# Causal attention inside a four-layer hybrid kernel: query preparation and normalising on GpSimd, and the mask of the maxima added by VectorE

## The chip, the cores and the metric

The kernel runs on one core of a Trainium2 chip. The metric is the device time of one execution in microseconds, lower is better. The core's engines are named as in the profile: PE (TensorE, matrix products), DVE (VectorE), ACT (ScalarE), POOL (GpSimd) and SP (SyncE, which here only issues transfers). They run their own instruction streams and meet at semaphores.

## The reference

Four layers follow each other, each `x = x + layer(layernorm(x))` on `x` of 4 x 1024 tokens of 128: a fast-weight attention, a mixture of experts, a causal attention, and the mixture of experts again. The change lies in the third. There `x` is seen as 2 batches of 256 in the layer's own text, but the shapes come from the argument, so it runs on 4 batches of 1024 tokens, with 16 heads of 8:

```python
def proj(W, b):
    y = jnp.einsum('bth,oh->bto', x, W) + b
    return y.reshape(B, T, nh, hs).transpose(0, 2, 1, 3)
Q, K, V = proj(Wq, bq), proj(Wk, bk), proj(Wv, bv)
Q = _apply_rope(Q, cos, sin)     # cos*even - sin*odd, the odd places zero
K = _apply_rope(K, cos, sin)
scores = jnp.einsum('bhqd,bhkd->bhqk', Q, K) * (1.0 / jnp.sqrt(hs))
scores = jnp.where(causal, scores, -10000000000.0)
att = jax.nn.softmax(scores, axis=-1)
y = jnp.einsum('bhqk,bhkd->bhqd', att, V)
return jnp.einsum('bth,oh->bto', y, Wo) + bo
```

## The kernel before, in words

`causal_attention_stage` is one block of five engine programs. A batch's 16 heads are four quads (`QUADS`, `QUAD`). Because the odd places after the rotation are zero, a head's rotated query and key have four numbers each (`ROT`). `rotate` multiplies the even half by the cosines and the odd half by the sines, `split` subtracts and writes the result as three bf16 parts; three `split`s give parts whose products add up to fp32 accuracy. ScalarE stacks the parts into rows (`stack_queries`, `stack_keys`), PE transposes the rows of a quad, and SP's transfers place the keys of each head (`place_keys`).

**Two passes over the scores.** The softmax needs the maximum of each query. So for each quad the scores are computed twice. First with the queries on the partitions: `max_step` makes a product of up to 512 keys in one of two PSUM buffers (`ps1`), and VectorE reduces it to one maximum (`maxima`, L1829, semaphores `s1_done` and `max_done`). A block of 128 queries j and a chunk c of 512 keys is a step; 12 steps (`MAX_STEPS`) of four heads make a quad, and in 8 of the 12 the last 128 columns lie on the diagonal: there a second product of the identity with a mask of -1e30 adds the causal mask (L1722). GpSimd splits the negated maxima in three bf16 parts too (`stack_maxima`) and they ride in the queries' rows, so that the second product gives score minus maximum. That one has the keys on the partitions (`exp_step`, two heads at a time in `ps2`, masked by a product as well, L1734); ScalarE takes the exponential, and `value_step` multiplies by the values in fp32.

**The slots.** A slot is one quad's 12 exponential steps. The maxima run ahead: step n of a slot also does maximum step n + 4 (`LEAD`) of the next quad, or, from n = 8 on, n - 8 of the one after. Within a step PE's order is: maximum product of head 0, exponential products of the first pair, head 1, second pair, head 2, then what stands under (n, "mid"), the value products of step n - 1, head 3, then what stands under (n, "end"). VectorE's order is the four reductions with the same places between. A maximum product waits until the buffer's last maximum but one is reduced (`max_done`), so each engine can be two maxima ahead of the other at most.

**The tables.** `COMMON`, `PREP`, `VALUES` and `OUTPUT` name what is done at the places: transposes of keys ("k") and queries ("q1", "q2"), of the output ("o0", "o1"), of the normalised input ("x0", "x1"), projections ("qk0" to "qk3", "v0", "v1"). All share one spare bank (`psm`) through `misc_full` and `misc_free`: who fills it waits until the last content was copied out, by ScalarE for k, q1, q2 and x, by VectorE for the rest.

**Preparing the next batch** is done in the slot of quad 1 (`prep`), in a loop over three batches; batch 0 is prepared before the first slot. VectorE takes the statistics of the layer norm at n = 1, GpSimd makes 1/sqrt(var + eps) (`rsqrt`), VectorE normalises at n = 3 (`normalize`, L1853: eight operations of 128 x 128), PE needs the result (`xn_done`) at "x0". After "qk3" VectorE rotates q (n = 10) and splits it in three pieces, at n = 11 and at n = 0 and 1 of the next slot, while GpSimd rotates and splits k. ScalarE waits for `q_split` at n = 2 and for `k_split` at n = 3 of quad 2's slot.

## Time and profile before

| | us |
|---|---|
| median of 3 runs | 1774.78 |
| lowest, highest run | 1768.44, 1775.36 |
| the profiled execution | 1769.27 |
| its span, first to last instruction | 1767.2 |
| attention stage in it, about | 787 to 1500 |

Times within a profile are microseconds from the span's start. A row of a timeline gives start, length, engine, line and operation, what it writes and reads, how many instructions were merged in it, and in brackets how long the engine had been idle before it and what released it. The length of merged instructions runs from the start of the first to the end of the last, and consecutive instructions of an engine overlap at their ends. Over the whole span PE is busy 69%, DVE 58%, ACT 36% and POOL 29%; these are averages over four layers with different limits, so the attention stage has to be read by itself.

### The profile page before, as it was taken

Reading aid. Unit: us, or ns where it says so; the run is one execution under the profiler, and the core shown is the slowest. Engines: PE = TensorE matmul, PEld = TensorE weight load, DVE = VectorE, ACT = ScalarE, POOL = GpSimd, SP = SyncE. Lnnn points to the kernel's source line nnn. Section 1 sums busy time; section 2 is a strip of 40 time slices with the busy share of each in tenths; the row PEclk is TensorE's granted clock in tenths of the full one; section 3 lists DMA queues with packets and bytes.
Section 4 is the critical chain, followed back from the end, with each engine's and each line's share of the span. In section 5 each row is a group of like instructions: output and inputs, shape, how many; then the busy total and the mean of one; then the engine's idle time right before and its main releaser. Section 6 shows DMA issues by size and latency. Waiting matters only on the chain. (4 is left out here: it accounts for less than half of the span.)

```text
span 1767.2 us, 26688 instructions
## 1 busy us (share of the span) xinstructions
PE 1212.8 (69%) x9140; PEld 801.2 (45%) x9214; DVE 1021.9 (58%) x2340; ACT 629.5 (36%) x989; POOL 510.0 (29%) x571
## 2 busy tenths in 40 slices
PE   4625977959635059704888998899889997412991
PEld 2413856839524059702343443344434443311991
DVE  5855555655426136446777776777777770630662
ACT  4632221222111023201265664665566665001330
POOL 2434013040026747712003000300120000374772
PEclk9666988969755579955699998999999998555995
DMA  1439611020120133160000010001000100213325
GB/s 45 155 145 390 266 37 59 0 95 0 36 63 28 53 106 99 52 185 6 7 19 7 10 46 8 7 7 43 8 7 8 31 7 13 62 53 90 98 68 162
DMA packets 109057, 114.06 MB, mean 65 GB/s; under 512 B 8720, under 2 KB 90512, under 8 KB 108048
## 3 DMA queue, kind: packets, MB, share of 16 engines
q1 hardware_dynamic: 96608, 91.98, 16.5%
q0 software_dynamic: 9216, 19.02, 3.2%
q10 hardware_dynamic: 3120, 1.57, 0.3%
q8 instruction: 68, 1.11, 0.3%
q14 instruction: 45, 0.37, 0.1%
HBM read 49.34 MB, written 59.02 MB: 61 GB/s over the span
## 5 line engine op out<-in xcount | busy, mean ns | idle before, releaser
L1829 DVE TENSOR_REDUCE att_mx<-att_ps 128x1 f32<-128x512 f32 (+3 forms) x768 | 405.2, 555 | 146.9 <-PE att_ps L1722 111.3
L1603 ACT ACTIVATE att_prob<-att_ps 128x1024 f32<-128x1024 f32 (+3 forms) x384 | 300.3, 812 | 228.9 <-PE att_ps L1734 176.7
L1719 PE MATMUL att_ps<-att_kT,att_q1T 128*128 128x512 bf16 (+3 forms) x709 | 235.1, 344 | 50.5 <-DVE att_mx L1829 34.2
L1731 PE MATMUL att_ps<-att_q2T,att_kT 128*128 128x512 bf16 (+3 forms) x753 | 201.1, 331 | 3.2 <-ACT att_prob L1603 1.2
L1719 PEld LDWEIGHTS att_ps<-att_kT,att_q1T 128*128 128x128 bf16 x768 | 74.2, 98 | 259.1 <-DVE att_mx L1829 211.7
L978 POOL DMA_INDIRECT sides<-moe_ys,moe_back_i x160 | 153.2, 958 | 87.6 <-issue 47.3
L1745 PE MATMUL att_pso<-att_prob,att_v 128*32 128x512 f32 (+3 forms) x1536 | 163.9, 499 | 1.6
L972 POOL DMA_INDIRECT slots<-moe_rows,moe_place_i x128 | 123.2, 963 | 59.4 <-issue 38.4
L1499 POOL CAST att_qm_rows<-att_nm 128x32 bf16<-128x32 f32 x48 | 15.6, 324 | 395.8 <-DVE att_nm L1838 391.6
L1722 PE MATMUL att_ps<-att_mask,att_identb 128*128 128x128 bf16 x512 | 115.8, 228 | 2.3 <-DVE att_mx L1829 1.5
L1071 PE MATMUL moe_ps_t<-moe_ident,moe_xs 128*128 128x128 f32 x160 | 27.0, 290 | 115.2 <-DMA moe_xs<-slots 115.2
L1734 PE MATMUL att_ps<-att_mask,att_identb 128*128 128x128 bf16 x512 | 102.4, 221 | 1.4 <-ACT att_prob L1603 0.8
L1018 ACT ACTIVATE moe_gated<-moe_ps_g 128x512 f32<-128x512 f32 (+1 forms) x96 | 50.6, 527 | 131.0 <-PE moe_ps_u L1086 131.0
L1265 DVE TENSOR_TENSOR moe_hid<-moe_gated,moe_ps_u 128x512 f32<-128x512 f32 (+1 forms) x96 | 57.4, 598 | 64.0 <-ACT moe_gated L1018 62.4
L1731 PEld LDWEIGHTS att_ps<-att_q2T,att_kT 128*128 128x128 bf16 x768 | 72.3, 99 | 47.7 <-ACT att_prob L1603 13.2
L1096 PE MATMUL moe_ps_y<-expert_wd,moe_hid 128*128 128x128 f32 x640 | 78.8, 275 | 0.0
L1096 PEld LDWEIGHTS moe_ps_y<-expert_wd,moe_hid 128*128 128x128 f32 x640 | 77.5, 191 | 2.7
L1071 PEld LDWEIGHTS moe_ps_t<-moe_ident,moe_xs 128*128 128x128 f32 x160 | 20.6, 151 | 115.8 <-issue 115.5
L1009 ACT ACTIVATE moe_xT_hi<-moe_ps_t 128x512 fp32r<-128x512 f32 (+1 forms) x48 | 25.1, 522 | 127.3 <-PE moe_ps_t L1071 127.3
L461 POOL TENSOR_TENSOR fw_wn<-fw_ssq,fw_half 128x20 f32<-128x20 f32 x3 | 10.6, 3532 | 202.1 <-DVE fw_ssq L668 202.1
L1230 DVE SCALAR_TENSOR_TENSOR moe_empty<-moe_xs,moe_spare_token 128x5 f32<-128x5 f32 x32 | 5.4, 176 | 109.7 <-DMA moe_xs<-slots 109.7
L696 DVE TENSOR_TENSOR fw_A<-fw_banks,fw_block_ones 128x512 f32<-128x512 f32 x45 | 31.1, 692 | 62.9 <-PE fw_banks L630 62.9
(283 smaller groups left out, 2439.5 us busy)
## 6 DMA issues: line engine op xcount, KB each, us to landing
slots<-fw_zeros SPq DMA_DIRECT2D x2, 5200.0 KB, 30.1
moe_xs<-slots SPq DMA_DIRECT2D x16, 650.0 KB, 4.9
sides<-fw_zeros SPq DMA_DIRECT2D x2, 4096.0 KB, 35.3
moe_side<-sides SPq DMA_DIRECT2D x16, 512.0 KB, 6.2
tok<-prep_tok SPq DMA_DIRECT2D x4, 1536.0 KB, 5.4
turned<-prep_tT SPq DMA_DIRECT2D x4, 1536.0 KB, 8.7
fw_tok<-tok SPq DMA_DIRECT2D x4, 1536.0 KB, 10.4
fw_Tkv<-turned SPq DMA_DIRECT2D x4, 1024.0 KB, 6.7
```

Source lines behind the costliest of these rows:

```text
L972: pool.indirect_dma_start(slots, bass.IndirectOffsetOnAxis(ap=place_i[b][:, j, k:k + 1], axis=0), source, None).then_inc(slots_written, 16)
L978: pool.indirect_dma_start(sides, bass.IndirectOffsetOnAxis(ap=back_i[e % 2][:, j:j + 1], axis=0), ys[n % 4][:, j - first], None).then_inc( ...
L1018: nc.scalar.activation(gated[k][:, 0:size], ps_g[k][:, 0:size], ACT.Silu).then_inc(silu_done, 1)
L1096: last = nc.tensor.matmul(ps_y[n % 2][:, j], hid[n % 2][k][:, j * P:(j + 1) * P], wd[:, e, k], start=(k == 0), stop=(k == 1))
L1265: nc.vector.tensor_tensor(hid[n % 2][k][:, 0:size], gated[k][:, 0:size], ps_u[k][:, 0:size], ALU.mult).then_inc(hid_done, 1)
L1603: nc.scalar.activation(prob[(2 * n + pair) % 4][:, :, 0:size], ps2[pair][:, :, 0:size], ACT.Exp, scale=SCORE_SCALE).then_inc(exp_done, 1)
L1719: last = nc.tensor.matmul(out[:, 0:size], q1T[t % 2][:, j * P:(j + 1) * P], kT[t][h][:, 512 * c:512 * c + size], start=True, stop=not diag ...
L1722: last = nc.tensor.matmul(out[:, size - P:size], identb[:], mask[:, 0], start=False, stop=True)
L1731: last = nc.tensor.matmul(ps2[pair][:, h, 0:size], kT[t][2 * pair + h][:, i * P:(i + 1) * P], q2T[t % 2][:, first:first + size], start=Tru ...
L1734: last = nc.tensor.matmul(ps2[pair][:, h, 0:P], identb[:], mask[:, 1], start=False, stop=True)
L1745: last = nc.tensor.matmul(pso[32 * h:32 * h + 32, first:512], v1[:, i * HEADS + QUAD * t + h, :], prob[(2 * n + h // 2) % 4][:, h % 2, 0:5 ...
L1829: nc.vector.reduce_max(mx[:, c, j, h:h + 1], ps1[(n * QUAD + h) % 2][:, 0:size], AX.X).then_inc(max_done, 1)
```

## The change

Four things are done at once.

1. `rsqrt` on GpSimd goes on to normalise, eight `tensor_scalar`s into `xn`, and gives `xn_done` itself. `rstd_done` and VectorE's `normalize` go, for batch 0 too.
2. In the loop GpSimd rotates and splits q, then k, where it did k alone. VectorE's pieces for q go. For batch 0 the work stays divided as before.
3. Statistics are taken at n = 0, and "x0" to "qk3" move one step forward in `PREP`.
4. Maxima on the diagonal: the mask product goes from PE. VectorE uses `tensor_tensor_reduce`, which adds a row block `mask_end` (384 zeros, then the mask's 128 columns) to the scores, writes the sums back to PSUM and keeps their maximum. `mask_end` is filled once at the start. In the built program this is two instructions, the second of which reads the maximum out. Before each maximum, on the diagonal or not, the wait is an instruction of its own (`wait`), which also counts up a semaphore.

```diff
-        PREP = {(4, "mid"): "x0", (5, "mid"): "x1", (7, "mid"): "qk0", (8, "mid"): "qk1", (9, "mid"): "qk2", (10, "mid"): "qk3"}
+        PREP = {(3, "mid"): "x0", (4, "mid"): "x1", (6, "mid"): "qk0", (7, "mid"): "qk1", (8, "mid"): "qk2", (9, "mid"): "qk3"}
...
-                nc.gpsimd.tensor_tensor(rstd[:], vareps[:], negh[:], ALU.pow).then_inc(rstd_done, 1)
+                nc.gpsimd.tensor_tensor(rstd[:], vareps[:], negh[:], ALU.pow)
+                pool.drain()
+                for j in range(TILES):
+                    last = nc.gpsimd.tensor_scalar(xn[:, j], xb[:, j], mv[:, j, 0:1], rstd[:, j:j + 1], ALU.subtract, ALU.mult)
+                last.then_inc(xn_done, 1)
...
-                    rotate(nc.gpsimd, 1)
-                    for n in range(3):
-                        last = split(nc.gpsimd, 1, n)
-                    last.then_inc(k_split, 1)
+                    for k, done in ((0, q_split), (1, k_split)):
+                        rotate(nc.gpsimd, k)
+                        for n in range(3):
+                            last = split(nc.gpsimd, k, n)
+                        last.then_inc(done, 1)
...
-                    last = nc.tensor.matmul(out[:, 0:size], q1T[t % 2][:, j * P:(j + 1) * P], kT[t][h][:, 512 * c:512 * c + size],
-                                            start=True, stop=not diagonal)
-                    if diagonal:
-                        last = nc.tensor.matmul(out[:, size - P:size], identb[:], mask[:, 0], start=False, stop=True)
-                    last.then_inc(s1_done, 1)
+                    nc.tensor.matmul(out[:, 0:size], q1T[t % 2][:, j * P:(j + 1) * P], kT[t][h][:, 512 * c:512 * c + size],
+                                     start=True, stop=True).then_inc(s1_done, 1)
...
-                    dve.wait_ge(s1_done, G * (STEPS * QUAD) + (n * QUAD + h + 1))
-                    nc.vector.reduce_max(mx[:, c, j, h:h + 1], ps1[(n * QUAD + h) % 2][:, 0:size], AX.X).then_inc(max_done, 1)
+                    wait(dve, s1_done, G * (STEPS * QUAD) + (n * QUAD + h + 1))
+                    scores, largest = ps1[(n * QUAD + h) % 2][:, 0:size], mx[:, c, j, h:h + 1]
+                    if P * (j + 1) == 512 * c + size:
+                        nc.vector.tensor_tensor_reduce(scores, scores, mask_end[:, 512 - size:512], 1.0, MASKED, ALU.add, ALU.max, largest).then_inc(max_done, 1)
+                    else:
+                        nc.vector.reduce_max(largest, scores, AX.X).then_inc(max_done, 1)
...
-                    if S.prep and n == 1:
+                    if S.prep and n == 0:
                         statistics(S.b + 1)
-                    if S.prep and n == 3:
-                        normalize(S.b + 1)
-                    if S.prep and n == 10:
-                        dve.drain()
-                        rotate(nc.vector, 0)
-                    if S.prep and n == 11:
-                        split(nc.vector, 0, 0)
-                    if S.t == 2 and S.more2 and n < 2:
-                        last = split(nc.vector, 0, n + 1)
-                        if n == 1:
-                            last.then_inc(q_split, 1)
...
+            nc.vector.memset(mask_end[:, 0:512 - P], 0.0)
+            nc.vector.tensor_copy(mask_end[:, 512 - P:512], mask_f[:, 0])
```

GpSimd in the loop's prepared slot, from the last cast of the maxima on: before, k alone (`att_turned`, `att_parts` are written once for k).

```order
L1505 ISA
L1415 REGISTER_ALU
L1464 TENSOR_TENSOR att_turned<-att_qkv,att_cs 128x512 x2
L1470 TENSOR_TENSOR att_turned<-att_turned 128x512
L1472 CAST att_parts<-att_turned 128x128x4
L1470 TENSOR_TENSOR att_turned<-att_turned,att_parts 128x512
L1472 CAST att_parts<-att_turned 128x128x4
L1470 TENSOR_TENSOR att_turned<-att_turned,att_parts 128x512
L1472 CAST att_parts<-att_turned 128x128x4
L1415 ISA
L1509 TENSOR_TENSOR att_res<-att_res,att_bo 128x1024
```

After the change the same place begins with q's five kinds of rows, and k's follow.

```order
L1473 CAST att_parts<-att_turned 128x128x4
L1471 TENSOR_TENSOR att_turned<-att_turned,att_parts 128x512
L1473 CAST att_parts<-att_turned 128x128x4
L1465 TENSOR_TENSOR att_turned<-att_qkv,att_cs 128x512 x2
L1471 TENSOR_TENSOR att_turned<-att_turned 128x512
L1473 CAST att_parts<-att_turned 128x128x4
L1471 TENSOR_TENSOR att_turned<-att_turned,att_parts 128x512
L1473 CAST att_parts<-att_turned 128x128x4
```

These are the end of q's rows and the beginning of k's: k's first multiplication stands behind all of q's, and the addition to `att_res` behind both.

PE in the same slot, from the transposes of the keys to the first projection. Before, the queries' transposes lie between the keys' transposes and qk0 (L1707), and a mask product (`att_mask,att_identb`) follows each maximum of a diagonal step. The piece shown begins at the queries' transposes; qk0 comes one more maximum later.

```order
L1667 MATMUL att_psm<-att_identb,att_q_rows 128x128 x8
L1718 REGISTER_ALU
L1719 MATMUL att_ps<-att_kT,att_q1T 128x512
L1722 MATMUL att_ps<-att_mask,att_identb 128x128
L1729 REGISTER_ALU
L1731 MATMUL att_ps<-att_q2T,att_kT 128x512 x2
L1718 REGISTER_ALU
L1719 MATMUL att_ps<-att_kT,att_q1T 128x512
L1722 MATMUL att_ps<-att_mask,att_identb 128x128
```

After:

```order
L1673 MATMUL att_psm<-att_identb,att_k_rows 128x128 x8
L1723 REGISTER_ALU
L1724 MATMUL att_ps<-att_kT,att_q1T 128x512
L1731 REGISTER_ALU
L1733 MATMUL att_ps<-att_q2T,att_kT 128x512 x2
L1723 REGISTER_ALU
L1724 MATMUL att_ps<-att_kT,att_q1T 128x512
L1731 REGISTER_ALU
L1733 MATMUL att_ps<-att_q2T,att_kT 128x512 x2
L1723 REGISTER_ALU
L1724 MATMUL att_ps<-att_kT,att_q1T 128x512
L1702 REGISTER_ALU
L1713 MATMUL att_psm<-att_wqkv,att_xT 128x256 x2
```

qk0 (now L1713) stands three maxima behind the keys' transposes, in the same bank; before, it stood three maxima behind the queries' transposes. The products with `att_mask` are gone from the maxima.

VectorE at the start of that slot. Before, the statistics stand behind the second step's maxima:

```order
L1828 REGISTER_ALU
L1829 TENSOR_REDUCE att_mx<-att_ps 128x1
L1842 ISA
L1844 BN_STATS att_stats<-att_xb 128x6 x8
L1847 BN_AGGR att_mv<-att_stats 128x2 x8
L1828 REGISTER_ALU
L1829 TENSOR_REDUCE att_mx<-att_ps 128x1
```

After, they stand behind the first step's, and the diagonal maxima that follow are pairs, an add-maximum (`att_ps,att_mx<-att_ps,att_mask_end`) and a read-out (`att_mx`):

```order
L1835 TENSOR_REDUCE att_mx<-att_ps 128x1
L1848 ISA
L1850 BN_STATS att_stats<-att_xb 128x6 x8
L1853 BN_AGGR att_mv<-att_stats 128x2 x8
L1416 REGISTER_ALU
L1833 ISA att_ps,att_mx<-att_ps,att_mask_end 128x128
L1833 ISA att_mx 128x1
L1416 REGISTER_ALU
L1833 ISA att_ps,att_mx<-att_ps,att_mask_end 128x128
L1833 ISA att_mx 128x1
```

The reduction before was one instruction with its wait inside; the waits, which this listing doesn't show, are now instructions between the rows.

## Rows read from the trace of the kernel before

**Rows 1.** Page, part 2: busy tenths of 40 slices of 44.2 us

```profile
PEclk9666988969755579955699998999999998555995
```

**Rows 2.** DVE by form: line, form, xcount | busy us, mean ns | idle

```profile
L1829 DVE TENSOR_REDUCE att_mx<-att_ps 128x1 f32<-128x512 f32 x384 | 253.2, 688 | 52.1 <-PE att_ps L1719 24.8 <-PE att_ps L1722 23.1
...
L1829 DVE TENSOR_REDUCE att_mx<-att_ps 128x1 f32<-128x256 f32 x128 | 53.0, 422 | 27.2 <-PE att_ps L1722 23.2
...
L696 DVE TENSOR_TENSOR fw_A<-fw_banks,fw_block_ones 128x512 f32<-128x512 f32 x45 | 31.1, 692 | 62.9 <-PE fw_banks L630 62.9
L701 DVE SCALAR_TENSOR_TENSOR fw_T<-fw_A,fw_eyes 128x512 f32<-128x512 f32 x45 | 30.8, 685 | 1.4
```

**Rows 3.** Timeline of PE in a plain step of 256 columns

```profile
1189.08 0.27 PE L1719 MATMUL att_ps<-att_kT,att_q1T 128*128 128x256 bf16 x1
1189.19 0.22 PE L1722 MATMUL att_ps<-att_mask,att_identb 128*128 128x128 bf16 x1
...
1190.94 0.28 PE L1719 MATMUL att_ps<-att_kT,att_q1T 128*128 128x256 bf16 x1
...
1191.80 0.34 PE L1719 MATMUL att_ps<-att_kT,att_q1T 128*128 128x384 bf16 x1
```

**Rows 4.** Timeline of DVE: maxima, aggregations, and a small operation

```profile
1079.86 0.64 DVE L1847 BATCH_NORM_AGGREGATE att_mv<-att_stats 128x2 f32<-128x6 f32 x8
...
1122.65 2.53 DVE L1829 TENSOR_REDUCE att_mx<-att_ps 128x1 f32<-128x512 f32 x4
...
1186.18 0.17 DVE L1833 TENSOR_TENSOR att_mx<-att_mx 128x16 f32<-128x16 f32 x1
1186.43 0.18 DVE L1838 TENSOR_SCALAR att_nm<-att_mx 128x32 f32<-128x32 f32 x1
...
1191.32 2.02 DVE L1829 TENSOR_REDUCE att_mx<-att_ps 128x1 f32<-128x256 f32 x4 [0.84 <-PE att_ps L1722]
```

**Rows 5.** Timeline of PE: its long waits for DVE in preparing slots

```profile
955.43 0.39 PE L1719 MATMUL att_ps<-att_kT,att_q1T 128*128 128x512 bf16 x1 [1.46 <-DVE att_mx L1829]
...
1088.42 0.60 PE L1701 MATMUL att_psm<-att_ident,att_xn 128*128 128x128 f32 x4 [2.06 <-DVE att_mx L1829]
...
1118.82 0.39 PE L1719 MATMUL att_ps<-att_kT,att_q1T 128*128 128x512 bf16 x1 [2.09 <-DVE att_mx L1829]
...
1128.21 0.23 PE L1719 MATMUL att_ps<-att_kT,att_q1T 128*128 128x128 bf16 x1 [2.25 <-DVE att_mx L1829]
```

**Rows 6.** Timeline of DVE: the preparing work of batch 1

```profile
1085.40 2.14 DVE L1853 TENSOR_SCALAR att_xn<-att_xb,att_mv,att_rstd 128x128 f32<-128x128 f32 x8
...
1110.58 0.69 DVE L1870 TENSOR_TENSOR att_qkv<-att_psm,att_bias 128x512 f32<-128x512 f32 x1 [0.49 <-PE att_psm L1707]
...
1125.28 2.18 DVE L1470 TENSOR_TENSOR att_turned<-att_turned,att_parts 128x512 f32<-128x512 f32 x1
```

**Rows 7.** Timeline of POOL: rstd, k's rotation and split, a cast

```profile
1081.09 1.67 POOL L1486 TENSOR_TENSOR att_rstd<-att_vareps,att_negh 128x8 f32<-128x8 f32 x1 [0.15 <-issue]
...
1115.10 2.52 POOL L1464 TENSOR_TENSOR att_turned<-att_qkv,att_cs 128x512 f32<-128x512 f32 x2 [8.02 <-DVE att_qkv L1870]
...
1123.99 0.61 POOL L1472 CAST att_parts<-att_turned 128x512 bf16<-128x512 f32 x1
...
1186.78 0.32 POOL L1499 CAST att_qm_rows<-att_nm 128x32 bf16<-128x32 f32 x1 [28.04 <-DVE att_nm L1838]
```

**Rows 8.** Stretch: us, PE, PEld, DVE, ACT, POOL busy (x), PEclk, DMA share, GB/s

```profile
1080.00:1120.00 40.00, 32.99 (x249) 16.21 (x254) 29.33 (x67) 18.33 (x25) 8.82 (x12) 0.96 0.03 8
```

**Rows 9.** POOL by form, as rows 2

```profile
L1472 POOL CAST att_parts<-att_turned 128x512 bf16<-128x512 f32 x12 | 8.4, 703 | 1.6
...
L1484 POOL TENSOR_SCALAR att_vareps<-att_mv 128x8 f32<-128x8 f32 x4 | 1.0, 242 | 60.3 <-DVE att_mv L1847 60.3
```

**Rows 10.** Timeline of ACT: the first stacking of k

```profile
1135.71 1.47 ACT L1587 ACTIVATE att_k_rows<-att_parts 128x1536 bf16<-128x1536 bf16 x1
```

**Rows 11.** Waits of PE, 1080 to 1150: total us, times, longest

```profile
PE att_psm L1707 <- ACT att_q1T L1558: 1.1, 1, 1.1
```

More of the change, by code:

```diff
@@ L1301, in causal_attention_stage @@
         mask = sb("mask", [P, 2, P], BF16)
+        mask_end = sb("mask_end", [P, 512])
         cs = sb("cs", [P, TILES, 2, ROT])
@@ L1342, in causal_attention_stage @@
         x_loaded, res_loaded, res_biased, x_stored = sem("x_loaded"), sem("res_loaded"), sem("res_biased"), sem("x_stored")
-        stats_done, rstd_done, xn_done, q_split, k_split = sem("stats_done"), sem("rstd_done"), sem("xn_done"), sem("q_split"), sem("k_split")
+        stats_done, xn_done, q_split, k_split = sem("stats_done"), sem("xn_done"), sem("q_split"), sem("k_split")
         q_stacked, k_stacked, q_copied, k_placed, v_placed = sem("q_stacked"), sem("k_stacked"), sem("q_copied"), sem("k_placed"), sem("v_placed")
@@ L1716, in max_step @@
                     out = ps1[(n * QUAD + h) % 2]
-                    diagonal = P * (j + 1) == 512 * c + size
                     pe.wait_ge(max_done, u + 1)
-                    last = nc.tensor.matmul(out[:, 0:size], q1T[t % 2][:, j * P:(j + 1) * P], kT[t][h][:, 512 * c:512 * c + size],
-                                            start=True, stop=not diagonal)
-                    if diagonal:
-                        last = nc.tensor.matmul(out[:, size - P:size], identb[:], mask[:, 0], start=False, stop=True)
-                    last.then_inc(s1_done, 1)
+                    nc.tensor.matmul(out[:, 0:size], q1T[t % 2][:, j * P:(j + 1) * P], kT[t][h][:, 512 * c:512 * c + size],
+                                     start=True, stop=True).then_inc(s1_done, 1)
             def exp_step(G, t, n, pair):
@@ L1848, in statistics @@
                 last.then_inc(stats_done, 1)
-            def normalize(batch):
-                dve.wait_ge(rstd_done, batch + 1)
-                for j in range(TILES):
-                    last = nc.vector.tensor_scalar(xn[:, j], xb[:, j], mv[:, j, 0:1], rstd[:, j:j + 1], ALU.subtract, ALU.mult)
-                last.then_inc(xn_done, 1)
             def consume(use, count, t, batch):
@@ L1918, in _ @@
             nc.vector.memset(k_rows[:], 0.0)
-            normalize(0)
             for zeros in [q_rows] + qm_rows:
```

## The prediction

> **What bounds the kernel now.** First the page's strip of the granted clock [rows 1]: the attention stage lies in slices 19 to 33, about 820 to 1460 us, and there the clock is 9 tenths or more in nearly all slices (2.4 GHz). Outside the stage the change touches nothing. A stretch of it shows PE busy 33 of 40 us and DVE 29 [rows 8]; matmul ends are modelled, so that doesn't settle who waits. Next comes a timeline of one plain step [rows 3, 4].
>
> A step on PE is: max product 0, exp pair 0, max 1, exp pair 1, max 2, value products, max 3. Max 1 of the next step writes the PSUM buffer of this step's max 3, so it waits for DVE's reduction of that. In the step of 256 columns, max 1 starts at 1189.08, max 3 at 1190.94, DVE's reduction at 1191.32, and the next max 1 at 1191.80. The reduction takes 0.42 [rows 2], so it ends at 1191.74 and PE moves 0.06 later. The loop of 2.72 us is 1.86 of PE work, 0.38 from max 3 to DVE, 0.42 of DVE and 0.06 back. PE idles only about 0.15 of it: the stage is bound by a loop through both engines, with PE alone a short way behind. DVE alone is further behind: four reductions of 512 in a row take 2.53 [rows 4], so they start (2.53 - 0.69) / 3 = 0.61 apart, 2.45 for a widest step.
>
> Then the slots that prepare the next batch. There PE stops for DVE: 2.06 us for xn, 2.09 and 2.25 behind q's rotation and split, and 1.46 for the same in batch 0 [rows 5]. DVE's own rows name the work [rows 6]: 2.14 us of normalising, and one subtraction that took 2.18.
>
> **The change, part by part.** The sum is made against the profiled execution, 1769.3 us (span 1767.2). The runs' median, 1774.8, is 5.5 above it and the fastest run 0.8 below; I forecast on the profile's scale.
>
> *Normalising leaves DVE (3 loop batches).* PE's wait of 2.06 goes if GpSimd has xn in time. Before, GpSimd had rstd at 1082.76 [rows 7]. The statistics that it waits for, of 1079.86 [rows 4], now come a step (3 us) earlier: rstd at 1079.8. The eight tensor_scalars on GpSimd aren't in the trace. The nearest rows are 242 ns for 8 elements and 703 ns for a cast of 512 [rows 9]: by elements 0.35 each, 2.8 in all, at most 5.6. So xn is there at 1082.6, and PE wants x0 a step earlier than before, 1086.36 - 3.0 = 1083.4. No wait; with 5.6 a wait of 2.0, as before. Taken: -2.06 x 3 = -6.2, range -6.2 to 0. At the stage's start nothing hides it, and 2.8 stands for 2.14: +0.7 (up to +3.5).
>
> *q's rotation and split leave DVE.* PE's stops of 2.09 and 2.25 fall away, and a third: batch 0 shows 1.46, while batch 1 instead ran that stretch at 1.2 GHz, which took as much. 5.80 x 3 = -17.4. Batch 1 also fell to 1.2 GHz after its wait for xn; its 40 us window has a mean of 0.96 of full clock [rows 8], which is 3.2 us at half speed and costs 1.6: -1.6 once.
>
> *GpSimd does q, then k.* For k it took from 1115.10 to 1124.60, 9.5 us [rows 7]; its start waits for the last qk projection, which is now read a step earlier, when qk2 was (1110.58 + 0.69 [rows 6]). So q is done near 1120.9 and k near 1130.4, with a margin since DVE no longer runs beside it. ScalarE took k at 1135.71 [rows 10]; less the stops that go (5.8) it wants it at 1129.9. q has over 3 us in hand, k is late by 0.5: +1.5 for three batches, range 0 to +6. Behind that wait on ScalarE stand the exponentials, and PE and DVE behind those. add_output_bias and the next queries' copy, queued behind k on GpSimd, aren't needed before.
>
> *The projections move a step earlier.* qk0 now follows k's transposes in the one spare PSUM bank, not q1's. PE waited 1.1 us for ScalarE to copy q1 out before qk0 [rows 11]. Now it does so twice, after k and after q1: +1.2 x 3 = +3.6 (0 to +3.9).
>
> *PE loses 512 mask products.* Each holds PE 0.06 (1189.19 to the next product, 0.05 by its 128 columns) [rows 3]. The loop holds three of them (max 1, 2 and 3): -0.16 a step.
>
> *DVE's maximum becomes a wait, an add-maximum and a read-out.* The add-maximum reads PSUM and SBUF; an addition or product of that form takes 692 ns for 512, the reduction 688 [rows 2], so the main instruction is even. The read-out of one element isn't in the trace. From below: eight aggregations take 0.64 with 0.152 each, so 0.07 apart [rows 4]. From above: the small operation at 1186.43 starts 0.25 after its predecessor's start at 1186.18, behind a drain. I take 0.07, because nothing drains between; it comes before max_done, so it is in the loop. The wait is now an instruction of its own for every maximum: from 0 to 0.17 (GpSimd, which waits in this way, starts its cast at 1186.78, 0.17 after nm's end at 1186.61 [rows 4, 7]). I take 0.02, since it only shows when DVE is early.
>
> There are 192 steps of four maxima, 128 on the diagonal; 16 (12 diagonal) are in the prologue, where I count 0. In the rest: 116 x (-0.16 + 0.07) = -10.4, the waits 176 x 0.02 = +3.5. Where the widest maxima meet the shortest exponentials, the same loop with that step's widths comes to 2.65 (an estimate, a column at 1/2.4 ns), while DVE alone needs 4 x 0.70 = 2.8: +0.15 in each of 14 slots, +2. Together -5; break-even at 0.16 for read-out and wait.
>
> Sum: 1769.3 - 6.2 + 0.7 - 17.4 - 1.6 + 1.5 + 3.6 - 5 = 1744.9.
>
> Two-source vector operations on fp32 run at one element a cycle here, with one source in PSUM (692 ns) and with both in SBUF (685) [rows 2]. Neither keeps an accumulator. The Trainium skill, Vector Engine (DVE) Microarchitecture Reference, section Points that are easy to get wrong, says that scalar-tensor-tensor with two non-bf16 SBUF sources runs at half throughput, as no port is left for accumulator read-back. No row here shows that form, and the new one has only one source in SBUF; by the rule as it is written the sum stands, by its reason the second rival would come.
>
> **The rivals.**
> *Read-out and wait at their upper bounds.* 0.25 + 0.17 against 0.16 saved: +0.26 x 116 = +30, and the 60 other steps at +0.17 = +10: 1769.3 - 19.4 (all but the masks) + 40 = **1790**. With the wait at 0.05 the kernel is slower than before from a read-out of 0.26 on ((0.26 + 0.05 - 0.16) x 116 + 0.05 x 60 = 20). For it: two rows of that size. Against: both have a drain or another engine in them.
> *The add-maximum at half rate.* Then 512 elements cost 0.53 more, 384 0.40, 256 0.27. DVE alone would bind: 4 x 1.23 = 4.9 a step against loops of 3.1 and 2.7 for the two widest, 3.9 against 3.0 and 2.7, 2.8 against 2.2 and 2.6 (estimates, as above): with the narrow ones +7 a slot, in 176 / 12 = 14.7 slots, +103: 1769.3 - 19.4 + 103 = **1853**. Against: the 692 and 685 ns. The reason of the skill's rule just named would give this time.
> *GpSimd is late.* xn at its upper price (PE waits 2.0) and k 1 us later, three times: +9: **1754**. This is the new wait in the place of the one removed. For it: both margins are under 1 us.
> *PE alone binds the diagonal steps*, and all four masks count: 116 x -0.21 = -24, and no more than that from DVE: 1769.3 - 19.4 - 24 = **1726**. For it: PE idles only 0.15 in the step shown; against: the loop still has the 0.07.
>
> **How the numbers follow.** Forecast 0.52, upper bounds 0.16, half rate 0.06, GpSimd late 0.14, PE alone 0.12. Predicted 1745 us. Half rate and the top of the first rival are left out of the range: 1727 to 1775. Half a per cent (9 us, about what a measurement of this kernel can tell) from the median 1774.8: below 1766 lie forecast, GpSimd late and PE alone, 0.78, less 0.02 for the unforeseen, 0.76; of the first rival's 0.16 half is within, so same 0.10; slower 0.14.
>
> **What would show it.** Right: no PE wait over 1.5 us for DVE in preparing slots, two waits of about 1.2 before projections; add-maxima of about 690 ns at 512, followed by rows that start 0.6 after them and end by 0.76; plain slots 0.4 us shorter. Wrong: add-maxima near 1.2 us; plain slots longer than before; PE waiting for xn, or ScalarE for k; a granted clock under 1.0 in plain slots, since PE has less to do.

## The result: 0.4% slower, and the profile after

The changed kernel takes 1777.75 us in the median against 1771.54 for the kernel before on the same chip (15 runs each). The ratio is 1.0037, with a 95% interval of 1.0026 to 1.0047. Its profiled execution took 1778.23 us with a span of 1776.3, 9 more than the 1769.27 and 1767.2 of before. Forecast was 1745, with a range that ended at 1775: wrong in sign and outside the range.

The clock strip of after's page stands at 9 tenths or more in slices 20 to 33, where [rows 1] has two slices of 8. Falls of a few microseconds don't show in slices of 44 us:

```profile
PEclk8666988969755579855699999999999999555996
```

VectorE's maxima in after, by form over the whole span (columns as in [rows 2]):

```profile
L1835 DVE TENSOR_REDUCE att_mx<-att_ps 128x1 f32<-128x512 f32 x256 | 172.8, 690 | 39.8 <-PE att_ps L1724 32.7 <-remote 2.2 <-issue 1.8
L1833 DVE CUSTOM_DVE_ANT_0 att_ps<-att_ps,att_mask_end 128x512 f32<-128x512 f32 x128 | 87.9, 704 | 13.1 <-PE att_ps L1724 10.1
L1833 DVE DVE_READ_ACCUMULATOR2_ANT att_mx<- 128x1 f32 x512 | 72.4, 141 | 0.1
```

The add-maximum of 512 columns takes 704 ns, not the 1.2 us of the half-rate rival. Two in a row in the timeline of DVE, in a plain slot of after:

```profile
1189.13 0.70 DVE L1833 CUSTOM_DVE_ANT_0 att_ps<-att_ps,att_mask_end 128x512 f32<-128x512 f32 x1
1189.75 0.14 DVE L1833 DVE_READ_ACCUMULATOR2_ANT att_mx<- 128x1 f32 x1
1189.78 0.70 DVE L1833 CUSTOM_DVE_ANT_0 att_ps<-att_ps,att_mask_end 128x512 f32<-128x512 f32 x1
1190.40 0.14 DVE L1833 DVE_READ_ACCUMULATOR2_ANT att_mx<- 128x1 f32 x1
1190.53 0.70 DVE L1833 CUSTOM_DVE_ANT_0 att_ps<-att_ps,att_mask_end 128x512 f32<-128x512 f32 x1
```

The read-out starts 0.62 after the main instruction and ends 0.76 after it, as forecast (0.6 and 0.76). So neither the half rate nor a dear read-out came, yet plain slots became longer. The negated maxima are taken once a slot. Their rows give, for each kernel, first and last start (columns: line, engine, operation, count: shortest, median, longest ns, first and last start in us). In this order they are before, after, and six of the kernels below: waits, mask, no_product, q_norm, q_only, early.

```profile
L1838 DVE TENSOR_SCALAR att_nm<-att_mx x16: 181/181/182, 861.4 to 1457.0; 128x32 f32<-128x32 f32 x16
L1844 DVE TENSOR_SCALAR att_nm<-att_mx x16: 181/181/182, 869.1 to 1467.2; 128x32 f32<-128x32 f32 x16
L1838 DVE TENSOR_SCALAR att_nm<-att_mx x16: 181/181/182, 863.5 to 1478.6; 128x32 f32<-128x32 f32 x16
L1839 DVE TENSOR_SCALAR att_nm<-att_mx x16: 181/181/182, 868.0 to 1480.5; 128x32 f32<-128x32 f32 x16
L1834 DVE TENSOR_SCALAR att_nm<-att_mx x16: 181/181/183, 859.0 to 1450.0; 128x32 f32<-128x32 f32 x16
L1843 DVE TENSOR_SCALAR att_nm<-att_mx x16: 181/181/183, 864.6 to 1451.1; 128x32 f32<-128x32 f32 x16
L1839 DVE TENSOR_SCALAR att_nm<-att_mx x16: 181/181/182, 860.0 to 1447.8; 128x32 f32<-128x32 f32 x16
L1839 DVE TENSOR_SCALAR att_nm<-att_mx x16: 181/181/182, 862.4 to 1432.3; 128x32 f32<-128x32 f32 x16
```

The sixteen starts cut the stage into fifteen intervals. Eight are plain (no preparing, clock at 1.00 in all kernels) and tell the price of the masks. The seven kernels whose plain slots have the same code (before, q_norm, q_only, start_dve, table_back, early and spread) lie between 293.3 and 295.0 there, so a price can be read to about 0.2 a slot. Three pairs hold the preparing of a batch. "First maximum" and "first negated" are counted from the stage's first statistics. q_only2 is a second run of the kernel q_only.

| us | first maximum | first negated | first to last | eight plain intervals | the three preparing pairs |
|---|---|---|---|---|---|
| before | 45.7 | 76.5 | 595.7 | 293.4 | 86.0, 93.0, 89.1 |
| after | 50.0 | 82.4 | 598.1 | 300.5 | 83.0, 89.2, 88.4 |
| waits | 45.8 | 78.9 | 615.1 | 303.7 | 88.2, 93.0, 92.8 |
| waits2 | 45.9 | 81.5 | 631.8 | 312.3 | 91.4, 95.2, 94.6 |
| mask | 45.7 | 79.3 | 612.5 | 300.8 | 88.0, 93.3, 93.4 |
| no_product | 45.6 | 74.8 | 591.0 | 285.8 | 85.8, 92.3, 92.7 |
| after_nd | 50.0 | 82.4 | 592.5 | 296.6 | 82.8, 88.8, 87.4 |
| q_norm | 50.0 | 80.8 | 586.5 | 293.3 | 82.0, 88.6, 86.7 |
| q_only | 45.7 | 76.5 | 587.8 | 294.9 | 84.4, 86.1, 88.2 |
| q_only2 | 45.7 | 77.0 | 589.1 | 295.0 | 84.4, 87.8, 86.0 |
| start_dve | 45.7 | 75.2 | 591.2 | 294.8 | 82.0, 90.5, 88.7 |
| table_back | 45.7 | 76.5 | 591.5 | 295.0 | 83.2, 88.8, 88.6 |
| early | 45.8 | 76.5 | 569.8 | 294.8 | 77.7, 81.2, 80.3 |
| spread | 45.7 | 75.2 | 574.0 | 294.3 | 78.8, 83.2, 82.4 |

In after, then: +4.3 before the first maximum, +1.7 more to the first negated one, +7.1 in eight plain intervals (0.89 each), +2.8 in the first interval, where full clock is granted from 885 on instead of 871, and -7.5 in the three pairs with the masks' share in them, where without it -20 was forecast. The first interval also differs by 1.6 between the two profiles of the one kernel q_only, so its +2.8 is no firm price. The profiled execution also reached the stage 1.8 later than before's, and was 1.2 quicker behind the last negated maxima, both in code that is the same. Together that is the 9 us of the span.

PE's long waits in the preparing slot of batch 1, from the timeline of PE in after (they answer to [rows 5]):

```profile
1087.63 0.23 PE L1724 MATMUL att_ps<-att_kT,att_q1T 128*128 128x128 bf16 x1 [1.83 <-DVE att_mx L1833]
1096.13 0.54 PE L1707 MATMUL att_psm<-att_ident,att_xn 128*128 128x128 f32 x3 [2.44 <-POOL att_xn L1490]
1108.02 0.70 PE L1713 MATMUL att_psm<-att_wqkv,att_xT 128*128 128x256 f32 x2 [1.17 <-ACT att_kT_all L1571]
1113.59 0.48 PE L1713 MATMUL att_psm<-att_wqkv,att_xT 128*128 128x256 f32 x1 [1.06 <-ACT att_q1T L1564]
1155.25 0.23 PE L1724 MATMUL att_ps<-att_kT,att_q1T 128*128 128x128 bf16 x1 [0.84 <-DMA att_kT<-att_kT_all]
```

The stops of 2.09 and 2.25 behind q's work are gone. The two waits of about 1.2 before projections are there. But PE still waits for xn, now for GpSimd: 2.44 here, and 1.00 in each of the other two batches. The first row is the stop behind the statistics. It was 1.69 in before too, once a batch, and the prediction's list of stops lacks it.

### The profile page after: what moved, and what is told of

It is laid out like the page before. It is cut to its first block and busy times, and to the rows that moved or that the text cites. A ratio compares the mean times of both kernels' runs of the same rounds, so it can differ in the third digit from the quotient of the medians.

```text
span 1776.3 us, 26950 instructions
## 1 busy us (share of the span) xinstructions
PE 1202.1 (68%) x8635; PEld 778.6 (44%) x8702; DVE 1027.1 (58%) x2798; ACT 631.0 (36%) x989; POOL 554.9 (31%) x627
## 5 line engine op out<-in xcount | busy, mean ns | idle before, releaser
L1833 DVE CUSTOM_DVE_ANT_0 att_ps<-att_ps,att_mask_end 128x384 f32<-128x384 f32 (+3 forms) x512 | 250.8, 501 | 105.9 <-PE att_ps L1724 94.6
L1835 DVE TENSOR_REDUCE att_mx<-att_ps 128x1 f32<-128x512 f32 x256 | 172.8, 690 | 39.8 <-PE att_ps L1724 32.7
L1736 PE MATMUL att_ps<-att_mask,att_identb 128*128 128x128 bf16 x512 | 102.2, 221 | 1.1 <-ACT att_prob L1609 0.8
L1733 PEld LDWEIGHTS att_ps<-att_q2T,att_kT 128*128 128x128 bf16 x768 | 74.4, 98 | 40.1 <-ACT att_prob L1609 13.2
L1096 PE MATMUL moe_ps_y<-expert_wd,moe_hid 128*128 128x128 f32 x640 | 78.8, 275 | 0.0
L1833 DVE DVE_READ_ACCUMULATOR2_ANT att_mx<- 128x1 f32 x512 | 72.4, 141 | 0.1
```

The costliest lines, as they stand in the source:

```text
L1096: last = nc.tensor.matmul(ps_y[n % 2][:, j], hid[n % 2][k][:, j * P:(j + 1) * P], wd[:, e, k], start=(k == 0), stop=(k == 1))
L1733: last = nc.tensor.matmul(ps2[pair][:, h, 0:size], kT[t][2 * pair + h][:, i * P:(i + 1) * P], q2T[t % 2][:, first:first + size], start=Tru ...
L1736: last = nc.tensor.matmul(ps2[pair][:, h, 0:P], identb[:], mask[:, 1], start=False, stop=True)
L1833: nc.vector.tensor_tensor_reduce(scores, scores, mask_end[:, 512 - size:512], 1.0, MASKED, ALU.add, ALU.max, largest).then_inc(max_done, 1)
L1835: nc.vector.reduce_max(largest, scores, AX.X).then_inc(max_done, 1)
```

## Experiments on the masks and the waits

Ratios are to the kernel before on the same chip, with their 95% intervals. The chip of after_nd, waits2, start_dve and table_back ran the kernel before in 1847.8 us instead of 1771, so those four are compared by ratio, or by the intervals of the stage. The kernel before has no profile from that chip.

**mask**: the kernel before with item 4 alone. 

> The kernel before with the mask part of the change alone: mask products off PE, add-maximum and read-out on VectorE, a wait of its own before each maximum. Theory (read-out and wait outweigh the products saved): in the trace of after the plain slots are 0.8 us longer than before and the prologue up to the first negated maxima 1.7 longer, so 14.7 x 0.8 + 1.7 = +13 against the kernel before. Rival (my prediction's term): -5. Rival (the +9 of the whole comes from elsewhere, GpSimd's normalising above all): within 3 of the kernel before.

Measured: ratio 1.0105 (1.0089 to 1.0122), +19 us. Eight plain intervals +7.5, so 0.93 a slot. The masks' part loses, and more than the whole change does.

**waits**: nothing but the wait. `wait` waits and counts up a semaphore; in the built program that is one instruction of VectorE's sequencer. A wait without the count wasn't tried.

```diff
-                    dve.wait_ge(s1_done, G * (STEPS * QUAD) + (n * QUAD + h + 1))
+                    wait(dve, s1_done, G * (STEPS * QUAD) + (n * QUAD + h + 1))
```

> The kernel before with only one thing of the change: the wait before each of VectorE's 768 maxima is an instruction of its own. Theory A (the wait costs only when VectorE is early, 0.02 a step as in the prediction): +3.5. Theory B (the wait is most of the masks' loss): +8 to +13, since the four maxima of a step each start 0.05 or more later. Theory C (the read-out is all of the loss): 0 to +1.

Measured: 1.0112 (1.0096 to 1.0128), +19 to +20 us, and 1.29 a plain slot, which is 0.107 a step. This single line costs as much as the whole mask part; even Theory B was below it. The stage's first two maxima show the price alone, with PE's second mask product and then VectorE. Before:

```profile
830.29 0.31 PE L1722 MATMUL att_ps<-att_mask,att_identb 128*128 128x128 bf16 x1
830.64 0.51 DVE L1829 TENSOR_REDUCE att_mx<-att_ps 128x1 f32<-128x128 f32 x2 [9.14 <-PE att_ps L1722]
```

With the wait of its own (run waits):

```profile
829.98 0.31 PE L1722 MATMUL att_ps<-att_mask,att_identb 128*128 128x128 bf16 x1
830.44 0.51 DVE L1829 TENSOR_REDUCE att_mx<-att_ps 128x1 f32<-128x128 f32 x2 [9.26 <-PE att_ps L1722]
```

From the product's start to the reduction's 0.35 became 0.46. The trace has the wait instruction itself too: it starts at 830.33, as long behind the product as the reduction did before, and the reduction follows 0.11 later. The reductions themselves take as long, and where they follow each other without a gap they lie as close as before (0.61 apart at 512 columns); the 0.11 is paid only where VectorE is waiting. In before it is idle for over 0.15 us ahead of at least one maximum in 158 of the 192 steps, in the loop that sets the pace, and the mean price of a step is one such 0.11.

**waits2**: the same, with one more semaphore count between wait and reduction.

```diff
                     wait(dve, s1_done, G * (STEPS * QUAD) + (n * QUAD + h + 1))
+                    dve.sem_inc(waits_passed, 1)
```

> The kernel before with the waits of their own, as in the run waits, and one more semaphore count of VectorE behind each of them, ahead of the reduction. Theory A (each instruction between the wake-up and the reduction costs its own time in the loop): about as much again as the first, +10 to +19 over the run waits, 1800 to 1809. Theory B (the price is of waking up once, whatever follows): within 3 of the run waits.

Measured: 1.0218 (1.0196 to 1.0240), another 1.06% on the 1.12% of waits, 8.5 more in eight plain intervals (1.07 a slot, 0.09 a step). Theory A: the price isn't of waking once; a second instruction between the wake-up and the operation costs about as much again. The pair of rows as above:

```profile
871.65 0.31 PE L1722 MATMUL att_ps<-att_mask,att_identb 128*128 128x128 bf16 x1
872.22 0.53 DVE L1830 TENSOR_REDUCE att_mx<-att_ps 128x1 f32<-128x128 f32 x2 [9.35 <-PE att_ps L1722]
```

Now 0.57. So 0.35, 0.46 and 0.57 with zero, one and two instructions in between: 0.11 each where VectorE waits. Two of them also show a little where it doesn't: reductions of 128 columns in a row start 0.24 apart, and 0.21 to 0.22 with one or none.

These rows fit a drawing of the Trainium skill, Perfetto Trace Analysis, section Per-engine timelines: an instruction that carries its wait is decoded and pushed into a wait queue beforehand, while one that the sequencer handles alone waits in the sequencer, and what follows is decoded only afterwards. The page gives no price for it; the 0.11 us is from these rows.

**no_product**: the kernel before without the second product of the maxima (the maxima then run over masked keys too), nothing in its place.

```diff
-                    if diagonal:
-                        last = nc.tensor.matmul(out[:, size - P:size], identb[:], mask[:, 0], start=False, stop=True)
```

> The kernel before without the mask products of the maxima, nothing in their place (so the maxima run over all keys of the block, masked ones too, and the output differs a little or not at all): waits of VectorE carried by the reductions, no read-out. It prices the products removed. Prediction's term: 0.16 a diagonal step in the loop, 116 x 0.16 = -18.6, 1.3 a plain slot. Theory: mask and waits differ by 0.36 a plain slot, the product saved less the read-out, so with a read-out of 0.13 a diagonal step (1.0 a slot) the product is worth 1.4 a slot: -19 to -20 with the prologue. Rival (PE's product lies beside DVE's work and saves 0.06 a step, as it takes once): -7.

Measured: 0.9917 (0.9899 to 0.9935), -14.7 us, 0.94 less in a plain slot, so 0.117 a diagonal step. Neither number expected was hit: at 0.055 a product, it counts about twice a step, not three times and not once. The read-out can be worked out from three differences, if the parts add up: mask less waits is -0.36 a slot, of which the product is -0.94, which leaves +0.58 for add-maximum and read-out, 0.072 a diagonal step, within about 0.03. It agrees with the 0.07 by which the read-out ends later than a reduction.

**after_nd**: the changed kernel, but the 4 of 12 steps off the diagonal get their embedded wait back.

```diff
-                    wait(dve, s1_done, G * (STEPS * QUAD) + (n * QUAD + h + 1))
+                    if P * (j + 1) == 512 * c + size:
+                        wait(dve, s1_done, G * (STEPS * QUAD) + (n * QUAD + h + 1))
+                    else:
+                        dve.wait_ge(s1_done, G * (STEPS * QUAD) + (n * QUAD + h + 1))
```

> The changed kernel, but the plain reductions off the diagonal (4 of a slot's 12 steps) carry their wait themselves again; the add-maxima keep the wait of their own. Theory (a wait of its own delays a maximum for which VectorE waits by 0.11 us, once in each step): 4 x 0.11 = 0.43 less in each of 14.7 slots and the prologue, -6 to -7 against the changed kernel, so 1771. Rival (the delay comes from the add-maxima's read-out and only they matter): -1 at most.

Measured: 1.0012 (0.9992 to 1.0032) against the changed kernel's 1.0037, and 3.9 less in eight plain intervals: 0.49 a slot where 0.43 was expected. That fits the theory in the changed kernel too. In whole runs it is weaker: the ratios differ by 0.25%, some 4 us for 6 to 7 expected, they come from two chips, and their intervals overlap. The add-maximum with a wait that it carries itself wasn't tried, and no run shows whether it can carry one. As an estimate from the prices above it would save 8 x 0.11 more a slot, and the masks' part would gain 0.36 a slot, some 5 us.

## Experiments on GpSimd's part

**q_norm**: the change without item 4. 

> The change without its mask part: q's rotation and split and the normalising on GpSimd, the table moved a step, mask products and maxima as before. Theory: normalising at the start +4.3 (GpSimd's eight take 6.3 us in the trace of after, VectorE's took 2.1); preparing slots +3.6 and -7.0 three times as in the trace of after, less the 0.8 of the masks in each: -15. Together -11 against the kernel before. Rival (my prediction's terms for these parts): -19. Rival (the parts lean on each other, so that the masks' part only costs because VectorE is fuller): 0.

Measured: 0.9976 (0.9965 to 0.9986), -4 to -5 us. In its profile the loop gives 9.2 (595.7 to 586.5), the start takes 4.3. Batch 0, POOL's timeline in after (the same length in q_norm), then VectorE's first projection:

```profile
789.67 1.68 POOL L1487 TENSOR_TENSOR att_rstd<-att_vareps,att_negh 128x8 f32<-128x8 f32 x1
791.52 6.32 POOL L1490 TENSOR_SCALAR att_xn<-att_xb,att_mv,att_rstd 128x128 f32<-128x128 f32 x8 [0.18 <-issue]
...
803.85 0.69 DVE L1870 TENSOR_TENSOR att_qkv<-att_psm,att_bias 128x512 f32<-128x512 f32 x1 [8.21 <-PE att_psm L1713]
```

Eight operations take 6.32 us, and nothing is there to lie beside it. By form they take 797 ns each:

```profile
L1490 POOL TENSOR_SCALAR att_xn<-att_xb,att_mv,att_rstd 128x128 f32<-128x128 f32 x32 | 25.0, 797 | 0.7 <-issue 0.7
```

VectorE took 2.14 for the same eight [rows 6]: GpSimd is three times slower at it, and its 0.80 each is over twice the 0.35 that I took. The Trainium skill, GPSIMD Engine Reference, section 4.1 Engine selection, has one-input elementwise operations on GpSimd at roughly line rate; for this tile of 128 x 128 the row doesn't agree, and the row decides.

**q_only**: as q_norm, but VectorE normalises, for batch 0 and in the loop (a step earlier than before). 

> As the one above, but VectorE normalises, a step earlier than before, for batch 0 as before. So only q's rotation and split move, and the table. Theory: the 4.3 at the start is not paid, and PE's wait for xn in the loop is VectorE's 2.1 in place of GpSimd's 6.3: 4.3 + 3 x 3 = 13 faster than the one above, -20 or more against the kernel before. Rival (in the loop normalising on either engine costs the same, since VectorE's 2.1 also holds up the maxima): 4.3 faster than the one above, -15.

Measured: 0.9938 (0.9923 to 0.9954), and 0.9942 (0.9925 to 0.9959) in a second run, q_only2, which stood beside the last two below. 

> The run q_only again, beside the two below, on their chip: 11 to 13 under the kernel before.

Together -9 to -13 us in the medians: already better than both kernels. First maximum back at 45.7; the loop gives 7.9 (6.6 in q_only2), hardly less than q_norm's 9.2. The rival came true as far as this can tell: in the loop the engine that normalises makes no difference that stands out. The reading is coarse, since start_dve below has the same loop code as q_norm and its loop took 4.7 more (591.2 against 586.5), 3.9 of it in the preparing pairs, where 3.4 more is lost to the lower clock. PE's waits for xn in q_norm's loop (total, times, longest):

```profile
PE att_psm L1706 <- POOL att_xn L1489: 4.7, 3, 2.6
```

With VectorE normalising (q_only), PE waits 1.82 three times behind it, 5.5 in all.

**start_dve**: as q_norm, with batch 0 alone normalised by VectorE. 

> As the run q_norm (q's rotation, split and the loop's normalising on GpSimd, mask products kept), but VectorE normalises batch 0 at the start. Theory: -4.3 against q_norm (the stage's first maximum 4.3 earlier) and a clock that rises as in q_only: 1758 to 1761. Against q_only, which normalises on VectorE in the loop too: -1, since PE's three waits for xn were 1.1, 2.6 and 1.1 there and 1.8 each here. Rival (the medians' 7.5 between q_norm and q_only came mostly from the loop): within 2 of q_norm.

Measured: 0.9947 (0.9928 to 0.9965), 0.3% under q_norm's ratio. The first maximum is at 45.7 instead of 50.0, as expected. Within its interval it is no better than q_only, and "-1 against q_only" can't be told.

**table_back**: as start_dve, with x0 to qk3 back where they were. 

> As start_dve, but x0 to qk3 stand where they stood in the kernel before; statistics stay a step earlier. Theory (the step earlier buys nothing, since GpSimd is in time either way): PE has xn without a wait (1.1 gone), and waits for ScalarE's copy once a batch instead of twice (1.17 gone): 3 x 2.2 = -6.7 against start_dve, less what k's later split costs at the stack: -3 to -7, 1752 to 1756. Rival (k a step later holds up ScalarE and all behind it): +3 to +6 against start_dve.

Measured: 0.9939 (0.9920 to 0.9958), the same as start_dve within the noise; neither number expected came, since what each side named is there and the two cancel. PE's waits for xn (6.2 in start_dve) and for k's copy (3.5) are gone. In their place stands, three times, this row (timeline of PE), and ScalarE's row says why:

```profile
1174.60 0.39 PE L1739 MATMUL att_ps<-att_q2T,att_kT 128*128 128x512 bf16 x1 [2.92 <-ACT att_prob L1611]
```

```profile
1172.15 1.48 ACT L1595 ACTIVATE att_k_rows<-att_parts 128x1536 bf16<-128x1536 bf16 x1 [2.98 <-POOL att_parts L1472]
```

GpSimd does q and k one after the other, k comes 3 us late, and the exponentials behind ScalarE's wait hold up PE. The step earlier in the table removes this stop and brings the other two back; in time it is worth nothing that this can tell.

**early**: as q_only, with statistics ahead of n = 0, normalising at n = 1, and this table:

```diff
-        PREP = {(3, "mid"): "x0", (4, "mid"): "x1", (6, "mid"): "qk0", (7, "mid"): "qk1", (8, "mid"): "qk2", (9, "mid"): "qk3"}
+        PREP = {(2, "mid"): "x0", (3, "mid"): "x1", (4, "mid"): "qk0", (5, "mid"): "qk1", (8, "mid"): "qk2", (9, "mid"): "qk3"}
```

> As q_only (VectorE normalises, GpSimd rotates and splits q and k, mask products), with another table: statistics ahead of n = 0, normalising at n = 1, x0 and x1 at n = 2 and 3, qk0 and qk1 at 4 and 5, ahead of k's and q1's transposes, qk2 and qk3 at 8 and 9, behind the output's. Theory: PE no longer waits for ScalarE's copies of k and q1 (1.17 and 1.05) and k is in time: 3 x 2.2 = -6.6 against q_only. Rival (statistics and normalising come closer together, so PE stops as long for them at another place, and the clock falls in the same way): within 2.

Measured: 1744.08 us, 0.9839 (0.9823 to 0.9856): 27 us under the kernel before and 18 under q_only2 beside it, nearly three times what was expected. Waits of PE from 860 on, q_only2:

```profile
PE att_ps L1720 <- DVE att_mx L1830: 19.1, 34, 1.8
PE att_psm L1708 <- ACT att_kT_all L1566: 3.5, 3, 1.2
PE att_psm L1708 <- ACT att_q1T L1559: 3.2, 3, 1.1
```

and early, where the other two have no row:

```profile
PE att_ps L1720 <- DVE att_mx L1830: 12.6, 33, 1.9
```

The 6.7 for ScalarE's copies are gone as expected. Another 6.5 of waits for VectorE went too, which I hadn't expected. Their rows tell where. In q_only2 PE stops in each batch behind the statistics and behind normalising; batch 1:

```profile
1078.97 0.23 PE L1720 MATMUL att_ps<-att_kT,att_q1T 128*128 128x128 bf16 x1 [1.72 <-DVE att_mx L1830]
1086.61 0.28 PE L1720 MATMUL att_ps<-att_kT,att_q1T 128*128 128x256 bf16 x1 [1.82 <-DVE att_mx L1830]
```

In early, batches 1 and 2 have no such stop behind the statistics. They now run just behind a stop of some 3 us at the start of the loop's turn, which all the kernels here have and which is no wait for VectorE:

```profile
1065.18 0.61 PE L1720 MATMUL att_ps<-att_kT,att_q1T 128*128 128x512 bf16 x1 [2.96 <-issue]
1065.28 1.64 DVE L1845 BATCH_NORM_STATS2 att_stats<-att_xb 128x6 f32<-128x128 f32 x8 [2.32 <-issue]
```

Batch 0 lacks that stop of 3 us, and there PE still waits 1.91 behind the statistics. Behind normalising, a step earlier than in q_only, two waits of 0.43 and 0.40 stand in all three batches instead of the 1.82. PE also loses less time to the lower clock: 3.4 us less in the preparing pairs. Together 16.6 of the 18; the rest isn't explained. Whether the order of early gains as much without q's move wasn't tried.

**spread**: as early, with statistics and normalising each in two halves, maxima between. 

> As early, but statistics and normalising are each cut in two halves with maxima between. Theory (a stop of PE is what of VectorE's 1.7 and 2.1 exceeds the two maxima that it may be ahead; halves of 0.8 and 1.1 stay mostly within): 3 x 2 = -6 against early, and one fall of the clock less per batch, -1.5 each at most. Rival (VectorE has no slack beside the maxima, and the sum of the stops is kept): within 1 of early.

Measured: 0.9875 (0.9859 to 0.9892), 6 us slower than early, 5.3 of it in the three pairs. Both expectations fell. Here the several short stops cost more than the long ones: PE's waits for VectorE's maxima grew from 12.6 in 33 to

```profile
PE att_ps L1720 <- DVE att_mx L1830: 17.6, 40, 1.4
```

## Why the prediction was wrong, point by point

- **What bounds the stage** was right: the loop through PE and VectorE. waits, waits2 and no_product each change one link of it by about 0.1 us, and the time of a step follows by as much.
- **"The wait is now an instruction of its own"** is the step that failed. I took 0.02 because "it only shows when DVE is early", and counted +3.5. But the same text had found a loop in which each engine waits for the other in every turn. A link of a loop is paid in full each turn. Measured 0.107 a step: 1.29 x 14.7 = 18.9, and 2.4 in the prologue, where I counted 0, so 21 where whole runs show 19 to 20. The upper bound, 0.17, held it, and 0.17 was from the one row of an engine that waits in this way; choosing the end near zero was the mistake.
- **The read-out** at 0.07: right (0.072, within about 0.03).
- **The mask products** at 0.16 a step: 0.117 measured. With the read-out, and no trace of the +2 for steps bound by VectorE, the sum of these is -0.36 x 14.7 = -5.3 where -8.4 was counted.
- **Normalising in the loop**, -6.2: the assumed "0.35 each, 2.8 in all, at most 5.6" failed. 6.2 to 6.3 lies outside the bound, which was eight times the 703 ns of a cast of 512 elements, an operation of another kind. q_norm's pairs are only 1.4 shorter in sum than q_only's (257.3 against 258.7), and 0.9 shorter than in its second run. So -1, and start_dve's 261.2 for the same loop as q_norm's says that even its sign isn't sure.
- **The start**, +0.7 with up to +3.5: +4.3, from the same price.
- **q's rotation and split**: the stops went. With clock, k and projections the terms were -13.9; q_only shortens the three pairs by 9.4 (9.9 in its second run). The projections' +3.6 and a k just in time are as forecast. The halves of the pairs show where the gain went. The second halves, where q's stops were, fell from 44.9 to 37.7 each, 21.5 in all. The first halves grew by 12.1 in sum. One of the four projections of each batch moved into them (1.1 of PE each, 3 in all, which the second halves gained), the waits for k's copy are 3.5, and time lost to the lower clock went from 5.1 to 10.2 (8.5 in the second run). In the second halves 3.4 of such loss went, so over whole pairs the clock gained nothing, where -1.6 was counted. What is left isn't settled.
- **Waits for the keys' transfers** weren't foreseen. PE's waits in the stage of after, and of before:

```profile
PE att_ps L1724 <- DMA att_kT<-att_kT_all: 7.6, 9, 1.3
```

```profile
PE att_ps L1719 <- DMA att_kT<-att_kT_all: 1.2, 2, 0.7
```

  The run waits has 3.5 in five, mask 5.6 in six, q_norm 1.4 in two. They come with the masks' part, and in part with its waits alone; the cost in the intervals above already holds them, and whether they add to it is open.

The corrected terms: waits +17.8 above forecast, products and read-out +3.1, xn +5.0, start +3.6, q's part +4.2, together 33.7 on 1744.9, which is 1778.6; the profiled execution took 1778.2. That fit is partly luck. Several terms are known only to a few microseconds at best (xn above all), 1.8 of the measured time came from ahead of the stage and 1.2 were regained behind it, and the parts don't quite add up: mask and q_norm multiply to 1.0081, after has 1.0037, some 8 us less. The intervals show where some of it lies: in the second half of each preparing pair the masks cost 1.1 to 1.5 on top of the kernel before, and 0.2 on top of q_norm (37.7 to 37.9 each time), 3 us in all. Why the waits cost nothing just there is open.

**The rivals.** The time, 1777.75, lies between the end of the range (1775) and the first rival, of waits and read-outs at their upper bounds, 1790: its wait was the true cause, its read-out was not. "Slower" had been given 0.14. "GpSimd is late" came true for xn. Its 1754 was a sum on top of masks that gain. The half rate fell with the 704 ns of the add-maximum, and "PE alone binds" with no_product, since more than one mask product a step but not all four counted. Of the signs of being wrong two came: longer plain slots, and PE waiting for xn.

## What to carry to other kernels

The advice here is what this one kernel bears out. Find the loop that sets the pace, and price every instruction that a change puts into it once per turn, waits and semaphore counts too; "it only shows when the engine is early" describes exactly the loops that matter. A wait that an operation can carry itself should stay in it, and an operation that is given one of its own costs that on top. Moving work to an idle engine pays where other work lies beside it (q, in the loop) and not where it stands alone (normalising at the start); and after such a move it was the order of the small steps around it, not the engine, that gave the largest gain (early).

## What the runs showed of the chip

- A wait (with a count) as an instruction of its own ahead of a VectorE operation adds 0.11 us when VectorE is waiting, and nothing visible when operations are queued back to back. A semaphore count behind it adds another 0.11 when VectorE is waiting.
- The combined add and maximum reads PSUM and SBUF in fp32 and writes PSUM at 704 ns for 512 columns (433 for 256, 299 for 128), against 690 for the plain maximum of 512, and its read-out takes another 141. So this two-source form with an accumulator, one source in PSUM, is not at half rate.
- GpSimd's tensor_scalar with two per-partition scalars takes 797 ns for 128 x 128 fp32, where its plain bf16 casts of 512 elements take 623 in the same trace.
- The clock doesn't follow from the length of PE's waits alone. Stretch of the preparing pair, with us, PE, PEld, DVE, ACT, POOL busy (x), PEclk, DMA share, GB/s, of batch 0 in before and in q_norm:

```profile
895.60:981.60 86.00, 72.13 (x589) 34.47 (x596) 66.90 (x145) 50.78 (x66) 17.52 (x23) 1.00 0.05 12
```

```profile
900.50:982.50 82.00, 73.52 (x586) 35.29 (x592) 57.82 (x129) 50.62 (x66) 30.41 (x39) 0.98 0.05 13
```

Before had 11 us of waits over 0.7 there and no fall of the clock; q_norm had 5 and fell to the lower level (1.2 GHz) for a while. The time lost to the lower clock (length x (1 - PEclk), summed over the fifteen intervals; the time spent at it is twice that) was 13.2 in before, 16.2 in q_norm, 14.9 and 15.7 in the two runs of q_only, 24.7 in table_back, 12.2 in early and 10.2 in spread, which is the slower of the last two. The profiled execution of table_back was the slowest of its six, so its figure may be above its usual one.
